# Row maxima carried into the stacked queries by one DMA per batch, in a four-layer cross-attention kernel

## The chip, the core and the metric

The kernel runs on one core of a Trainium2 chip. The metric is the device time of one execution in microseconds. The engines are TensorE (PE), VectorE (DVE), ScalarE (ACT), GpSimd (POOL) and SyncE (SP); SP and ACT also issue DMAs, each through a queue of its own.

## What is computed

Eight batches of 128 tokens and 128 features pass four attention layers, all f32, against a context of the same shape. Layers 0, 2 (with its cross part, "C") and 3 have 16 heads of 8 features; layer 1 has 16 heads of 64.

```python
# layer 0 (heads of 8, mask on the keys), then layer norm
scores = q @ k.T ; p = softmax(scores * scale + mask) ; x = LN(x + (p @ v) @ wo)
# layer 1 (heads of 64): x = x + attention(rms(x), ctx)
# layer 2: x = x + sa(LN(x))          causal, with a router that blocks 64-token blocks
#          x = x + ca(LN(x), ctx)     cross layer, C
#          x = x + relu(LN(x) @ w1 + b1) @ w2 + b2
# layer 3: x = LN(x + attention(x, ctx, ctx))
```

## The kernel before

**Exact products from bf16.** The 8-feature heads are too short for f32 matmuls to be cheap, so queries and keys are cut into three bf16 parts (`part_q`, `part_k`, with `rest_q`, `rest_k` between) and stacked: `qs` and `ks0`/`ks1` hold, for each head, 6 rows per feature slot (table `SLOTS`) in which a part stands opposite the part it must meet. The stacks are filled by DMAs (`stack_dma`, one per slot, six per group of batches) from SP's queue, for the first group of queries from ACT's. The seventh slot (`ROW_SLOT`) of `ks0` holds the mask (`kaug`) and meets ones in `qs`; the eighth is unused.

**The two passes.** The four attention parts 0, 2, C, 3 give 32 items (`N_ITEM`), one per batch and part, numbered n. For item n TensorE makes the scores with queries on the partitions (`pe_scores`, L311: 8 matmuls per half of the heads; the score pass). VectorE takes the negated row maxima (`dve_max`, L463). GpSimd cuts them into three bf16 parts (`pool_split`), TensorE turns them (`pe_mT`, L321), ScalarE copies them to `mrow` (`act_mrow`, L383). Then TensorE makes the scores a second time with keys on the partitions (L294; the shifted pass) and adds the maxima with 8 more matmuls of a selection matrix `sel` and `mrow` (L304), so that ScalarE's exponential (`act_exp`, L389) needs no bias per row. The probabilities then multiply the values (`pe_V`, L338), `act_osum` copies the result, `pe_back` turns it, `dve_norm` divides it by its sums, `pe_onT` turns it again, `act_onT` (L402) copies it, and `pe_z` (L355) multiplies it by the output matrix, `dve_z` adds the residual.

**Steps.** The order is written out by hand as steps s (`pe_attn`, `act_attn`, `dve_attn`, `pool_attn`). In step s the score pass of item s stands in both halves, with the second half of the shifted pass of item s-2 and the first half of that of item s-1; `pe_V` of item s-2 ends the step. Items from 24 on come one step later. `even` and `odd` put other work into the two halves: V chunks of layer 1 (`pe_v1`), projections, `pe_f1`, `pe_f2` and turns. Step 0 to 9 are layer 0; layer 1 (`pe_l1` and its like) follows with its own order; then steps 8 to 36 for layer 2, C and 3. The queries of an item of C or layer 3 come from the result of the layer before for the same batches, so each pair of batches has a chain: projection, parts, stack DMAs, score pass.

**Queues.** SP issues in the order of its program and waits for each part in turn: an issue behind a part that is not ready stands still. Input loads share the two queues with the stacks.

Of the kernel before, what the change touches and what calls it, by code (L numbers as in the profile page):

```python
# [7 lines left out]
P = 128  # L8
B = 8
# [27 lines left out]
ROW_SLOT = 6  # L37
HALVES = ((0, 4), (4, 4))
# [18 lines left out]
def build(nc, xt_d, x_d, ctxt_d, mask_d, wmat_d, wcol_d, wrow_d, out_d):  # L57
    ctx = ExitStack()
    with ctx:
# [50 lines left out]
        group = sb("group", [P, G])  # L110
        pick = sb("pick", [P, 8])
        sel = sb("sel", [P, 4, P], BF16)
# [14 lines left out]
        maskbc = xn[:, :, :].rearrange("p b t -> p (b t)")  # L127
        up = probs[:, 2, 0:HALF].bitcast(BF16).rearrange("p (b c) -> p b c", c=P)
# [91 lines left out]
        def data_of_S(n):  # L220
            L, b = layer(n), n % B
            return L.stacked("q", b) + L.stacked("k", b) + ([(sem("kaug_in"), 16)] if n == 0 else [])
# [14 lines left out]
        V1_EVEN = {1: (3,), 2: (6,), 3: (9,), 4: (11,), 5: (13,), 6: (15,)}  # L237
        V1_ODD = {0: (1, 2), 1: (4, 5), 2: (7, 8), 3: (10,), 4: (12,), 5: (14,)}
        freed(0, 1, sem("v_out_L1"), 1)
# [37 lines left out]
        def T_ready(e, n, half):  # L277
# [3 lines left out]
            if 2 * n + half:  # L281
                e.wait_ge(sem("exp_done"), 2 * n + half)

# [4 lines left out]
        def pe_scores(e, n, half, m, mhalf):  # L288

            if m is not None:  # L290
                M, b = layer(m), m % B
                T_ready(e, m, mhalf)
                for c, r, rows, i in heads(mhalf):
                    e.matmul(bank(4 + r)[:, bt(c)], ks[M.slot][rows, i, bt(b)], qs[rows, i, bt(b)],  # L294
                             start=(c == 0), stop=False, skip_group_check=True)
                if M is L2:
                    for a in range(2):
                        e.matmul(bank(4 + a), causal[:, :], identB[:, :].unsqueeze(1).broadcast_to([P, 4, P]),
                                 start=False, stop=False, skip_group_check=True)
# [23 lines left out]
        def pe_V(e, n):  # L323
            e.wait_ge(sem("exp_done"), 2 * n + 2)
            e.wait_ge(sem("vpad_in"), n + 1)
            if n >= 2:
                e.wait_ge(sem("z_read"), n - 1)
            if n == 0:
                e.wait_ge(*L0.v_done("v_out", 1))
            if n == 1:  # L330
# [1350 lines left out]
```

## Time and profile before

| | us |
|---|---|
| median of 3 runs | 361.03 (358.65 to 361.56) |
| profiled execution | 359.1 |
| its span | 357.3 |

| engine | busy us | share |
|---|---|---|
| PE, matmul | 308.4 | 86% |
| PE, weight load | 215.2 | 60% |
| DVE | 242.2 | 68% |
| ACT | 212.7 | 60% |
| POOL | 97.1 | 27% |

The span runs from the first to the last instruction. Busy shares are means over stages with different limits, so the stages are read apart. The first score pass starts at 19.48 us, step 2 at 31.05, layer 1 fills about 80 to 182, step 11 starts at 199.71, step 16 at 233.85, step 32 at 336.08. TensorE's granted clock is 0.981 of full speed over the span.

### The profile page before, as it was taken

The page shows a single profiled execution, that of the slowest core. Times are in us where ns is not written, and L with a number is a line of the kernel's source. Part 1 is how long each engine was busy: PE and PEld are TensorE (multiplying, and loading weights), DVE is VectorE, ACT ScalarE, POOL GpSimd, SP SyncE. Part 2 cuts the span into 40 slices and gives each one's busy share as a digit, 9 for nine tenths or more (in the row PEclk, how much of TensorE's full clock was granted, in tenths as well). Part 3 has the DMA queues.
Part 4 walks back from the last instruction along what each step waited for, and adds up shares of the span by engine and source line. Part 5 has one row for each costly group of instructions (what it writes and reads, how often), then busy time and mean ns, then how long its engine had stood idle before and what let it go on. Part 6 is the DMA issues. An engine that isn't in the chain of part 4 may idle for free.

```text
span 357.3 us, 10164 instructions
## 1 busy us (share of the span) xinstructions
PE 308.4 (86%) x4069; PEld 215.2 (60%) x4069; DVE 242.2 (68%) x478; ACT 212.7 (60%) x459; POOL 97.1 (27%) x263
## 2 busy tenths in 40 slices
PE   2779999997999999988879999989886977998871
PEld 0434566775778778867655556556654765775550
DVE  7656478628987467667657456868876647667755
ACT  2247767757785785876745645646574553556560
POOL 8011734310310000101405534233342313423231
PEclk9969999999999999999999999999999999999898
DMA  6447740000000000001311322412332010011000
GB/s 215 146 123 209 253 186 5 2 0 2 2 2 2 0 2 0 2 2 46 84 50 37 85 69 68 121 31 74 91 90 61 3 47 24 24 46 38 25 17 29
DMA packets 26158, 20.65 MB, mean 58 GB/s; under 512 B 3192, under 2 KB 24960, under 8 KB 25856
## 3 DMA queue, kind: packets, MB, share of 16 engines
q1 hardware_dynamic: 24656, 18.44, 17.6%
q10 hardware_dynamic: 1456, 1.58, 1.4%
q8 instruction: 32, 0.52, 0.6%
q14 instruction: 14, 0.11, 0.1%
HBM read 6.63 MB, written 0.52 MB: 20 GB/s over the span
## 4 chain that ended last, share of the span: by engine, by line
PE 50%; DVE 16%; ACT 12%; issue 6%; SPq 5%; DMA 5%; POOL 4%; ACTq 1%; POOLq 0%
SPq L653 5%; PE psum L338 5%; ACT probs L822 5%; PE psum L780 4%; DMA qs<-part_q 4%; PE psum L311 4%; PE psum L695 4%; PE psum L746 4%; PE psum L721 3%; ACT probs L830 3%; PE psum L294 3%; PE psum L304 3%; DVE maxs L463 3%; PE psum L757 2%; PE psum L941 2%
## 5 line engine op out<-in xcount | busy, mean ns | idle before, releaser
L463 DVE TENSOR_REDUCE maxs<-psum 128x8 f32<-128x1024 f32 x64 | 77.8, 1215 | 48.3 <-PE psum L311 32.2
L389 ACT ACTIVATE probs<-psum 128x1024 f32<-128x1024 f32 x64 | 65.5, 1023 | 36.5 <-PE psum L304 36.3
L311 PE MATMUL psum<-ks,qs 64*128 64x128 bf16 x512 | 26.0, 221 | 14.8 <-DMA qs<-part_q 8.0
L338 PE MATMUL psum<-probs,vpad 128*32 128x128 f32 x1024 | 35.4, 280 | 0.0
L822 ACT ACTIVATE probs<-psum,maxs 128x128 f32<-128x128 f32 x128 | 34.8, 391 | 0.5 <-DVE maxs L871 0.5
L338 PEld LDWEIGHTS psum<-probs,vpad 128*32 128x32 f32 x1024 | 26.7, 111 | 12.2 <-ACT probs L389 6.4
L441 POOL CAST mp<-maxs 128x16 bf16<-128x16 f32 x32 | 6.9, 216 | 91.1 <-DVE maxs L463 90.6
L524 POOL TENSOR_SCALAR rstd<-stats 128x2 f32<-128x2 f32 (+1 forms) x19 | 4.2, 223 | 100.6 <-DVE stats L490 100.5
L311 PEld LDWEIGHTS psum<-ks,qs 64*128 64x128 bf16 x512 | 15.1, 95 | 24.6 <-issue 9.7
L881 DVE TENSOR_REDUCE mres<-probs 128x8 f32<-128x1024 f32 x16 | 19.4, 1215 | 12.3 <-ACT probs L822 12.3
L871 DVE TENSOR_REDUCE maxs<-psum 128x8 f32<-128x1024 f32 x16 | 19.5, 1220 | 11.7 <-PE psum L746 11.7
L294 PE MATMUL psum<-qs,ks 64*128 64x128 bf16 x512 | 25.6, 220 | 0.6 <-ACT probs L389 0.6
L304 PE MATMUL psum<-mrow,sel 32*128 32x128 bf16 x512 | 25.3, 217 | 0.0
L294 PEld LDWEIGHTS psum<-qs,ks 64*128 64x128 bf16 x512 | 14.5, 94 | 13.6 <-issue 7.7
L304 PEld LDWEIGHTS psum<-mrow,sel 32*128 32x128 bf16 x512 | 14.4, 93 | 11.9 <-issue 6.6
L396 ACT COPY osum<-psum 128x256 f32<-128x256 f32 x32 | 12.0, 375 | 14.9 <-PE psum L338 14.6
L772 PE MATMUL psum<-probs,v1all 128*64 128x128 f32 x256 | 17.5, 279 | 3.4 <-ACT probs L830 2.9
L830 ACT COPY probs<-psum 128x1024 f32<-128x1024 f32 x16 | 16.7, 1042 | 6.2 <-PE psum L757 6.2
L885 DVE TENSOR_TENSOR probs<-probs,mres 128x1024 f32<-128x1024 f32 x16 | 19.6, 1225 | 0.6
L526 POOL TENSOR_TENSOR rstd<-rstd,small 128x2 f32<-128x2 f32 (+1 forms) x23 | 17.9, 780 | 1.9
L695 PE MATMUL psum<-wmat,ctxT 128*128 128x512 f32 x32 | 18.4, 676 | 0.0
L772 PEld LDWEIGHTS psum<-probs,v1all 128*64 128x64 f32 x256 | 13.7, 136 | 7.1 <-ACT probs L830 5.9
(154 smaller groups left out, 633.8 us busy)
## 6 DMA issues: line engine op xcount, KB each, us to landing
qs<-part_q SPq DMA_DIRECT2D x78, 64.0 KB, 2.0
ks<-part_k SPq DMA_DIRECT2D x30, 128.0 KB, 2.4
ks<-part_k SPq DMA_DIRECT2D x36, 64.0 KB, 2.0
wmat<-in_wmat SPq DMA_DIRECT2D x1, 1856.0 KB, 9.3
wmat<-in_wmat SPq DMA_DIRECT2D x1, 1024.0 KB, 5.1
qs<-part_q SPq DMA_DIRECT2D x6, 128.0 KB, 2.4
wrow<-in_wrow SPq DMA_DIRECT2D x1, 704.0 KB, 6.3
wmat<-in_wmat ACTq DMA_DIRECT2D x1, 512.0 KB, 8.2
```

The source lines that it names most:

```text
L294: e.matmul(bank(4 + r)[:, bt(c)], ks[M.slot][rows, i, bt(b)], qs[rows, i, bt(b)], start=(c == 0), stop=False, skip_group_check=True)
L304: mm = e.matmul(bank(4 + a)[:, bt(i)], sel[rg(j), i, :], mrow[rg(j), m % 2, :], start=False, stop=True, skip_group_check=True)
L311: s_mm = e.matmul(bank(2 * half + r)[:, bt(c)], qs[rows, i, bt(b)], ks[L.slot][rows, i, bt(b)], start=(c == 0), stop=L is not L2, skip_gro ...
L338: mm = e.matmul(o_bank(n)[rg(c), bt(half)], vpad[:, n % 2, 4 * half + c, G * a:G * a + G], pt, start=(a == 0), stop=(a == 1), skip_group_c ...
L389: e.activation(probs_of(n, half), bank(4, 2), ACT.Exp, scale=layer(n).scale)\
L463: e.tensor_reduce(maxs[:, n % 2, 8 * half:8 * half + 8], bank(2 * half, 2).rearrange("p (h k) -> p h k", k=P), AX.X, ALU.max, negate=True)\
L695: e.matmul(bank(to), ctxT[:, bt(c // 2)], mat("v1")[:, c % 2 * 512:(c % 2 + 1) * 512], start=True, stop=True).then_inc(L1("v_mm"), 1)
L772: mm = e.matmul(bank(6)[HD * pp:HD * pp + HD, bt(t)], v1[:, b, h * HD:(h + 1) * HD], pT[:, half, bt(4 * pp + t)], start=True, stop=True)
L822: ins = e.activation(probs[:, half, bt(s)], bank(2 * half, 2)[:, bt(s)], ACT.Exp, bias=maxs[:, b % 2, 8 * half + s:8 * half + s + 1])
L830: e.copy(pT[:, half, :], bank(4, 2)).then_inc(L1("pT_out"), 1)
L871: e.tensor_reduce(maxs[:, b % 2, 8 * half:8 * half + 8], bank(2 * half, 2).rearrange("p (h k) -> p h k", k=P), AX.X, ALU.max, negate=True)\
L885: e.tensor_tensor(p8, p8, rec.unsqueeze(2).broadcast_to([P, 8, P]), ALU.mult).then_inc(L1("norm"), 1)
```

## The change

The eighth slot (`MAX_SLOT`) of the keys' stacks now holds ones, and that of `qs` holds zeros during the score pass. When the maxima are turned and copied to `mrow`, ScalarE issues one DMA that writes them into this slot of `qs` for the batch. The shifted pass then adds them by itself; `sel`, `mrow`'s matmuls and the three VectorE instructions that made `sel` go. Because an item's maxima stay in the slot, it is cleared by a further DMA for each pair of queries of C and 3 (`clear_q`), and once for layer 2. Slot rows that fills of whole stacks wrote before are now filled by three DMAs from `resid` (`slots`), and the key stacks' fills between layers write ones instead of zeros.

The order moves with it. Both halves of item s-2's shifted pass stand in step s; `pe_V` is cut into halves at the end of step s and in the next; `pe_onT`, `act_onT` and `pe_z` of an item stand all in one step; the DVE order of `dve_norm`, `dve_z` and the second maximum changes. GpSimd waits for the mask parts before its fills. Values of layer 0 and V chunk 0 move behind the first score pass. The loads of the masks, `x`, `wrow`, `wcol`, `a1` and the rest of the weights move from SP's queue to ACT's, and `v1` from ACT's to SP's. SP issues key and query parts in turn.

```diff
+MAX_SLOT = 7
+            if n == 0:
+                ready += [(sem("kaug_in"), 16), (sem("slots"), 48)]
...
+            if half == 0:
+                e.wait_ge(sem(f"rows{n % 2}"), 16 * (n // 2 + 1))
...
-                e.wait_ge(sem("mT_read"), m + 1)
-                for i in range(4):
-                    for a in range(2):
-                        j = 2 * mhalf + a
-                        mm = e.matmul(bank(4 + a)[:, bt(i)], sel[rg(j), i, :], mrow[rg(j), m % 2, :],
...
+        ROWS_ON_ACT = range(N_ITEM)
+
+        def max_rows(e, n):
+
+            e.wait_ge(sem("mT_read"), n + 1)
+            e.dma_start(qs[MAX_SLOT::8, :, bt(n % B)], mrow[:, n % 2, :]).then_inc(sem(f"rows{n % 2}"), 16)
...
-                pe_scores(e, n, 0, n2, 1)
+                pe_scores(e, n, 0, n2, 0)
                 ahead(s)
                 if n1 is not None:
                     pe_mT(e, n1)
+                if n4 is not None:
+                    pe_onT(e, n4)
                 even(s)
                 if n3 is not None:
-                    pe_back(e, n3)
+                    pe_V(e, n3, 1)
                 if n4 is not None:
                     pe_z(e, n4)
-                pe_scores(e, n, 1, n1, 0)
+                pe_scores(e, n, 1, n2, 1)
                 if n3 is not None:
-                    pe_onT(e, n3)
+                    pe_back(e, n3)
                 odd(s)
                 if n2 is not None:
-                    pe_V(e, n2)
+                    pe_V(e, n2, 0)
...
+        def clear_q(e, L, b0, nb):
+
+            e.wait_ge(sem("exp_done"), 2 * B * (L.at - 1) + 2 * (b0 + nb))
+            e.dma_start(qs[MAX_SLOT::8, :, toks(b0, nb)], kaug[:, 0:nb * P]).then_inc(sem(f"q_clear{b0}"), 16)
...
+            e.wait_ge(sem("fill"), 2)
+            e.dma_start(ks0[MAX_SLOT::8, :, :], ones.bitcast(BF16)).then_inc(sem("slots"), 16)
+            e.dma_start(qs[ROW_SLOT::8, :, :], ones.bitcast(BF16)).then_inc(sem("slots"), 16)
+            e.dma_start(qs[MAX_SLOT::8, :, :], zeros.bitcast(BF16)).then_inc(sem("slots"), 16)
+            e.dma_start(wmat[:, c1:c2], wmat_d[:, c1:c2]).then_inc(sem("in_v1"), 16)
...
-            e.memset(qs[:, :, :].rearrange("p c t -> p (c t)").bitcast(F32), TWO_ONES).then_inc(sem("qs_one"), 1)
-            e.memset(wide_f32(ks0, 3), 0.0).then_inc(sem("ks0_zero"), 1)
+            e.wait_ge(sem("up"), 3)
...
-            e.memset(ks0[:, 0:4, :].rearrange("p c t -> p (c t)").bitcast(F32), 0.0).then_inc(sem("ks0_zero"), 1)
```

On TensorE, one middle step of layer 0 before, from its second shifted pass to the next step's:

```order
L304 MATMUL psum<-mrow,sel 128x128 x8
L311 MATMUL psum<-ks,qs 128x128 x8
L321 MATMUL psum<-identB,mp 128x128
L695 MATMUL psum<-wmat,ctxT 128x512
L346 MATMUL psum<-identF,osum 128x128 x2
L355 MATMUL psum<-wmat,onT 128x128
L294 MATMUL psum<-qs,ks 128x128 x8
L304 MATMUL psum<-mrow,sel 128x128 x8
L311 MATMUL psum<-ks,qs 128x128 x8
L351 MATMUL psum<-identF,onorm 128x128
L695 MATMUL psum<-wmat,ctxT 128x512
L338 MATMUL psum<-probs,vpad 32x128 x16
```

The same step now:

```order
L302 MATMUL psum<-qs,ks 128x128 x8
L313 MATMUL psum<-ks,qs 128x128 x8
L323 MATMUL psum<-identB,mp 128x128
L354 MATMUL psum<-identF,onorm 128x128
L722 MATMUL psum<-wmat,ctxT 128x512
L340 MATMUL psum<-probs,vpad 32x128 x8
L358 MATMUL psum<-wmat,onT 128x128
L302 MATMUL psum<-qs,ks 128x128 x8
L313 MATMUL psum<-ks,qs 128x128 x8
L349 MATMUL psum<-identF,osum 128x128 x2
L722 MATMUL psum<-wmat,ctxT 128x512
L340 MATMUL psum<-probs,vpad 32x128 x8
```

The matmuls on `sel` are gone, and the turn to `onT` (L351, now L354) stands at the head of the step whose `z` (L355, now L358) uses it, where before it stood half a step and a value pass earlier.

On ScalarE, the same step of layer 0 before:

```order
L396 COPY osum<-psum 128x256
L389 ACTIVATE probs<-psum 128x1024
L383 COPY mrow<-psum 128x128
L700 COPY v1all<-psum 128x512
L389 ACTIVATE probs<-psum 128x1024
L700 COPY v1all<-psum 128x512
L402 COPY onT<-psum 128x128
```

And now:

```order
L403 ACTIVATE probs<-psum 128x1024
L388 COPY mrow<-psum 128x128
L397 DMA qs<-mrow 16x8x128
L416 COPY onT<-psum 128x128
L727 COPY v1all<-psum 128x512
L410 COPY osum<-psum 128x256
L403 ACTIVATE probs<-psum 128x1024
```

The issue of the maxima's DMA stands between their copy and the copy of `onT`, which moved from the step's end to behind it.

On SP, the stacks of C and layer 3 before (512 columns are a group of four batches of keys, 256 a pair of queries):

```order
L653 DMA ks<-part_k 16x8x512 x12
L653 DMA qs<-part_q 16x8x256 x12
L653 DMA ks<-part_k 16x8x512 x6
L653 DMA qs<-part_q 16x8x256 x6
L653 DMA ks<-part_k 16x8x512 x6
L653 DMA qs<-part_q 16x8x256 x30
```

And now, down to the third pair of queries of C:

```order
L668 DMA ks<-part_k 16x8x512 x9
L674 DMA qs<-kaug 16x8x256
L668 DMA qs<-part_q 16x8x256 x6
L668 DMA ks<-part_k 16x8x512 x3
L674 DMA qs<-kaug 16x8x256
L668 DMA qs<-part_q 16x8x256 x6
L668 DMA ks<-part_k 16x8x512 x5
L674 DMA qs<-kaug 16x8x256
L668 DMA qs<-part_q 16x8x256 x6
```

The last part of a group of keys is issued behind a pair of queries instead of ahead of it, and a clearing DMA stands ahead of each pair.

## Rows read from the trace of the kernel before

**Rows 1.** Windows by stage: start:end, length, each engine's busy us (instructions), clock, DMA.

```profile
37.38:60.08 22.70, 22.36 (x369) 13.92 (x366) 16.23 (x37) 16.15 (x29) 11.76 (x28) 1.00 0.44 159
199.71:233.85 34.14, 34.14 (x511) 20.06 (x508) 22.65 (x44) 18.65 (x35) 13.20 (x39) 1.00 0.31 85
233.85:278.50 44.65, 37.63 (x664) 25.17 (x660) 34.09 (x68) 26.88 (x51) 15.86 (x49) 1.00 0.25 68
278.50:336.10 57.60, 50.32 (x812) 36.90 (x810) 37.88 (x82) 30.20 (x61) 16.66 (x53) 0.98 0.11 30
```

**Rows 2.** Waits of PE from 190 us on: total us, times, longest.

```profile
PE psum L311 <- DMA qs<-part_q: 8.0, 6, 2.5
PE psum L311 <- DVE rest_q L629: 2.7, 3, 1.1
```

**Rows 3.** Timeline of one step of layer 0: start, us, engine, instruction.

```profile
48.41 0.40 PE L294 MATMUL psum<-qs,ks 64*128 64x128 bf16 x8
...
48.74 0.40 PE L304 MATMUL psum<-mrow,sel 32*128 32x128 bf16 x8
...
49.18 1.02 ACT L389 ACTIVATE probs<-psum 128x1024 f32<-128x1024 f32 x1 [0.26 <-PE psum L304]
...
49.40 0.23 PE L321 MATMUL psum<-identB,mp 128*128 128x128 bf16 x1
...
49.46 1.08 PE L695 MATMUL psum<-wmat,ctxT 128*128 128x512 f32 x2
...
50.10 0.26 ACT L383 COPY mrow<-psum 128x128 bf16<-128x128 bf16 x1
50.38 0.38 PE L346 MATMUL psum<-identF,osum 128*128 128x128 f32 x2
...
53.02 1.08 PE L338 MATMUL psum<-probs,vpad 128*32 128x128 f32 x32
...
53.61 0.27 ACT L402 COPY onT<-psum 128x128 f32<-128x128 f32 x1
...
54.03 0.40 PE L294 MATMUL psum<-qs,ks 64*128 64x128 bf16 x8
```

**Rows 4.** The costliest groups: the matmuls that add the maxima.

```profile
L304 PE MATMUL psum<-mrow,sel 32*128 32x128 bf16 x512 | 25.3, 217 | 0.0
```

**Rows 5.** The line of the stacks, issues on ACT's queue: duration min/median/max in ns.

```profile
L653 ACTq DMA_DIRECT2D qs<-part_q x6: 614/622/768, 12.8 to 16.2; - x6
```

**Rows 6.** DMA issues: KB of each, median us from issue to landing.

```profile
qs<-part_q SPq DMA_DIRECT2D x78, 64.0 KB, 2.0
...
ks<-kaug SPq DMA_DIRECT2D x1, 256.0 KB, 3.2
...
xn<-in_mask SPq DMA_DIRECT2D x1, 128.0 KB, 6.3
...
r1p<-in_wmat SPq DMA_DIRECT2D x2, 32.0 KB, 8.0
...
wcol<-in_wcol SPq DMA_DIRECT2D x1, 9.0 KB, 2.7
```

**Rows 7.** Timeline of the start.

```profile
1.80 3.51 POOL L1019 MEMSET qs<- 128x4096 f32 x1
...
2.95 5.08 DVE L1452 CAST probs<-mu 128x128 bf16<-128x128 f32 x1
...
8.27 0.23 DVE L1456 CAST probs<-mu 128x128 bf16<-128x128 f32 x1
...
9.34 1.76 DVE L1462 MEMSET ks<- 128x2048 f32 x1 [0.38 <-issue]
...
11.02 0.36 DVE L585 TENSOR_TENSOR rest_k<-psum,xn 128x256 f32<-128x256 f32 x1
```

**Rows 8.** The chain that ended last, before step 22: the key part and the issues.

```profile
265.74 1.13 POOL part_k L641
267.46 0.60 SPq L653
```

More of the change, by code:

```diff
@@ L221, in data_of_S @@
             L, b = layer(n), n % B
-            return L.stacked("q", b) + L.stacked("k", b) + ([(sem("kaug_in"), 16)] if n == 0 else [])
+            ready = L.stacked("q", b) + L.stacked("k", b)
+            if n == 0:
+                ready += [(sem("kaug_in"), 16), (sem("slots"), 48)]
+            if n == B:
+                ready += [(sem("q_clear"), 32)]
+            if n >= 2 * B and b % 2 == 0:
+                ready += [(sem(f"q_clear{b}"), 16 * (n // B - 1))]
+            return ready
         FREED = {(0, 1): [(sem("kaug_out"), 1)],
@@ L321, in pe_mT, with pe_V @@
             e.transpose(m_turned(n), mp[:, n % 2, :], identB[:, :]).then_inc(sem("mT_mm"), 1)
[L323 to L330, printed above, removed]
[L331 to L340 removed]
+        def pe_V(e, n, half):
+            e.wait_ge(sem("exp_done"), 2 * n + half + 1)
+            if half == 0:
+                e.wait_ge(sem("vpad_in"), n + 1)
+                if n >= 2:
+                    e.wait_ge(sem("z_read"), n - 1)
+                if n == 0:
+                    e.wait_ge(*L0.v_done("v_out", 1))
+                if n == 1:
+                    e.wait_ge(*L0.mm_done("q_rest", 4))
+                if n == B:
+                    e.wait_ge(L1("z_read"), B)
+            for a in range(2):
+                for c in range(4):
+                    pt = probs_of(n, half)[:, bt(2 * c + a)]
+                    mm = e.matmul(o_bank(n)[rg(c), bt(half)], vpad[:, n % 2, 4 * half + c, G * a:G * a + G], pt,
+                                  start=(a == 0), stop=(a == 1), skip_group_check=True)
+            if half:
+                mm.then_inc(sem("V_mm"), 1)
         def pe_back(e, n):
@@ L405, in act_attn @@
             for s in steps:
-                n1, n2, n3 = at(s - 1, lo, hi), at(s - 2, lo, hi), at(s - 3, lo, hi)
+                n1, n2 = at(s - 1, lo, hi), at(s - 2, lo, hi)
+                n3, n4 = at(s - 3, lo, hi), at(s - 4, lo, hi)
+                first(s, 0)
+                if n2 is not None:
+                    act_exp(e, n2, 0)
+                if n1 is not None:
+                    act_mrow(e, n1)
+                if n4 is not None:
+                    act_onT(e, n4)
+                even(s)
                 if n3 is not None:
                     act_osum(e, n3)
-                first(s, 0)
+                first(s, 1)
                 if n2 is not None:
                     act_exp(e, n2, 1)
-                if n1 is not None:
-                    act_mrow(e, n1)
-                even(s)
-                first(s, 1)
-                if n1 is not None:
-                    act_exp(e, n1, 0)
                 odd(s)
-                if n3 is not None:
-                    act_onT(e, n3)
         def pool_v(e, n):
@@ L790, in pe_l1 @@
                 if b == 0:
+                    pe_onT(e, B - 1)
                     pe_z(e, B - 1)
@@ L1183, in _ @@
             pe_s1(e, 0, 1)
+            pe_onT(e, B - 2)
+            pe_V(e, B - 1, 1)
+            pe_z(e, B - 2)
             e.wait_ge(sem("exp_done"), 2 * B)
@@ L1186, in _ @@
             pe_back(e, B - 1)
-            pe_z(e, B - 2)
-            pe_onT(e, B - 1)
             def during1(b, place):
@@ L1441, in _ @@
             e.memset(up[:, :, :], 0.0).then_inc(sem("up"), 1)
+            e.memset(ones, TWO_ONES).then_inc(sem("fill"), 1)
+            e.memset(zeros, 0.0).then_inc(sem("fill"), 1)
             u = sem("mask_split")
```

187 lines of the change are left out of this document (93 added, 94 removed).

## The prediction

> **What bounds the kernel now.** I read the stage windows first [rows 1]. In layer 0 and in layer 2 TensorE is never idle: 22.36 busy of 22.70 us over steps 3 to 6, 34.14 of 34.14 over steps 11 to 15. So a step there lasts as long as its matmuls: 5.68 and 6.83 us. In the cross layer and layer 3 it is busy 37.63 of 44.65 and 50.32 of 57.60 us, that is 14.3 us idle. The waits of TensorE there [rows 2] put 8.0 us on the query stacks' transfers and 2.7 on VectorE's remainders. The stretch of layer 1 (80 to 182 us) holds none of the changed matmuls; I leave it as it is.
>
> One step of layer 0 [rows 3] shows what each piece takes. From 48.41 to 48.74 eight shifted-score matmuls pass (0.33 us), then the eight that add the maxima need the same 0.33 before the exponential starts at 49.18 and takes 1.02. The maxima copy takes 0.26, the step ends at 54.03: 5.62 us.
>
> **What goes.** All 512 matmuls on `sel` and `mrow` [rows 4]. Their 217 ns is the pipelined length; the spacing is 0.33 us for eight, so two halves cost 0.66 us per batch, 21 us over 32 batches. This is the ceiling of the steady gain, paid only where TensorE is what a step waits for.
>
> **What comes in its place, per batch.** ScalarE copies the turned maxima, waits for its own copy and issues a DMA. An issue on ScalarE's queue takes 0.61 to 0.77 us [rows 5]; with the wait I take 0.72. The transfer is 128 pieces of 256 bytes. No such transfer is in the trace. The query stacks (512-byte pieces, 64 KB) land in 2.0 us; the bias columns, 128 pieces of 72 bytes, in 2.7 [rows 6]. I take 2.0, as the size and the target tile are the same, and keep 2.7 as the bound; for less than 2.0 no row speaks. The Trainium skill (DMA: Bandwidth & Descriptors, Specifications) speaks against the change here: below 512 bytes a piece is read, modified and written, which would put the landing nearer to the 2.7 of the bias columns; by the row it is 2.0, by that reading some 0.7 more for each batch whose copy is waited for.
>
> Two loops follow from the new order.
>
> *The maxima loop.* Shifted pass 0.33, gap 0.11, exponential 1.02, copy 0.26, issue 0.72, landing 2.0, then the next batch's shifted pass: a step can't be shorter than 4.4 us. Layer 0, at 5.0 after the cut, and layer 2, at 6.2, lie above it, so there the transfer is hidden behind the second half of the step.
>
> *The late `onT`.* Before, ScalarE copied the turned output `onT` at the end of a step (53.61 in [rows 3]), and `pe_z` used it in the middle of the next, 2.5 us later. Now TensorE turns it at the head of a step, ScalarE copies it behind exponential, maxima copy and issue, and TensorE asks for it (`pe_z`) in the middle of the same step. Earliest: 0.33 + 0.11 + 1.02 + 0.26 + 0.72 + 0.27 + 0.1 = 2.8 us after the step's start. What TensorE has before it is two passes of 0.33, the turn of the maxima 0.07 (49.40 to 49.46), that of `onT` 0.2, the even filler, and 0.5 for half of the value pass (its whole is 53.02 to 54.03): 1.4 us plus the filler. The filler of layer 0 is a V chunk, 0.92 (49.46 to 50.38): wait 0.5. In layer 2, where both passes carry 0.54 of mask matmuls more, the wait is 0.8 in the steps without filler. In the cross layer and layer 3 it is 0.9 to 1.3 with a light filler, none with `pe_f2` or a full projection. Queued behind this wait are the second shifted and score passes, and so VectorE's second maximum.
>
> **The sum, stretch by stretch.**
>
> *Start.* The cast L1452 takes 5.08 us beside GpSimd's 3.51 us fill of `qs` and the fills behind it; its twin L1456 without them takes 0.23 [rows 7]. GpSimd now waits for the mask parts, and VectorE's 1.76 us fill of `ks0` is gone. That would free 4.85 + 1.76 = 6.6 us, but the first mask piece is issued at 1.6 and lands 6.3 later [rows 6], at 7.9, where L585 now starts at 11.02: 3.1 us. From L585 to the first scores the new order needs about 1.0 + 3.9 (six issues) + 0.6 + 3.2 (the `kaug` transfer [rows 6]) = 8.7, so 16.6 instead of 19.48. The three slot transfers (768 KB) and the 512 KB for `v1` ride ahead on the same queue and may eat all of that. From the first scores to step 2 (31.05 now, 11.6 us) the chain is two maxima 1.22 each behind the passes, GpSimd's split 1.4, turn, copy, issue and landing: 9.2. Sum -5.3; bounds 0 and -7.5.
>
> *Layer 0, steps 2 to 9.* Four steps have no such wait for `onT` (no `z` yet, or the 1.85 us chunks before it): 4 x -0.66; four have it: 4 x (-0.66 + 0.5). That is -3.3. The last value pass and its return come half a step later: +0.5. Together -2.8; bounds -5.3 and 0.
>
> *Layer 2.* Its first shifted pass now waits for copy, issue and landing (3.0 us) with only one score pass (0.9) and little else to cover it; less its own cut I charge +1.0. Steps 11 to 15: 5 x -0.66 + 0.8 x 3 - 0.3 = -1.2 with the waits partly covered by turns. With step 10's cut of 1.3: -1.5; bounds -4.6 and +1.
>
> *Cross layer and layer 3, steps 16 to 31.* Cut 15 x 0.66 = -9.9. The SP queue was in the way: at 265.74 GpSimd computes the last key part, at 267.46 the query stack's issues follow it [rows 8], though the query's first part, made in the step before, had been ready some 3 us. I lay 4.5 of the 8.0 us to this, which happened at steps 16, 20 and 22. The new order puts the late key parts behind the queries, and the added clearing DMA (some 0.6 us of SP) goes out before the part is ready, while SP is idle: -4.5. The other 8 us or so of short waits shrink by about half, since the new waits for `onT` stand in the same steps: -4.3. Against it nine light steps at +1.0: +9. In layer 3 the query stack is asked for one step after its projection, and that step gets shorter, so part of the cut turns into a wait there; I count it in the halving above. Sum -9.9 - 4.5 - 4.3 + 9.0 = -9.7; bounds -15 and -3.
>
> *End.* The last batch pays issue and landing in full, 2.7, less 0.33 of `sel`, some 0.5 of the value pass and some 0.5 as VectorE takes the second maximum before its other work: +1.3 (rounded); bounds +0.5 and +2.5.
>
> Sum: -5.3 - 2.8 - 1.5 - 9.7 + 1.3 = -18.0. The profiled execution took 359.1 us (span 357.3), so 341.1; the median of the three runs, 361.03, is 1.9 above it: **343 us**.
>
> **Rivals.**
> 1. *The wait for `onT` does not come* (ScalarE gets to it earlier, or the passes absorb it). Then the cut is whole: 0.5 x 4 in layer 0, 2 in layer 2, 4 more later, -8: 335. For it: TensorE has always other work queued; against: it is in order, and `z` stands ahead of the second pass.
> 2. *ScalarE's queue is the new bound.* Its waiting issue costs 1.2 us, not 0.72: the `onT` wait and both loops grow by 0.5 in some 20 steps, +10, or the start gives nothing (+5): 348 to 353. For it: in layer 0 ScalarE is busy 16.15 of 22.70 [rows 1] before the issue; against: the six issues in a row stay near 0.65.
> 3. *The row transfers land late* and the kernel gets slower. A step is then 2.4 + landing. It takes 18 us over 28 steps, 0.65 us on steps of about 5.8: from a landing of 4.0 us on the kernel is slower than before; at 4.5 it is 375. What speaks for it: a transfer behind a big load on the same queue waits for it, as `r1p` (32 KB) took 8.0 us behind the last load of `wmat` [rows 6], and exactly those loads move onto ScalarE's queue. The Trainium skill (DMA: Bandwidth & Descriptors, Queues, rings and completion order) says that each engine consumes one queue's descriptors in ring order; the row of `r1p` agrees. Against: they are issued one at a time (steps 3 and 5), and the next maxima follow about 5 us behind, when a load of that size is nearly down.
> 4. *It hardly moves*: the gains in the start and in the late layers are absorbed by other transfers, 357 to 364.
>
> **How the numbers follow.** Forecast (337 to 348) 0.52; rival 1 and better 0.15; rival 2 and a dull start 0.22; rival 4 0.05; rival 3 0.06. Range 333 to 354, which leaves out the two last and a thin slice of rival 1. Faster by over 1% (what a measurement of this kernel can tell) 0.89, within 1% 0.05, slower 0.06.
>
> **What would show it.** First scores at 16 to 17 us, and L1452's successor at 0.2 us. Layer 0 steps of 5.1 to 5.5 us with TensorE waiting about 0.5 for ScalarE's `onT` copy before `pe_z`; layer 2 steps near 6.6. ScalarE's row issues 0.6 to 0.8 us, landing 2.0 to 2.2, and no TensorE wait on them except for batches 0, 8 and the last. No wait over 1 us on `qs<-part_q` before steps 16, 20 and 22, but still one or two in layer 3. If steps in layers 0 and 2 are equal to before or TensorE waits for `qs<-mrow` in every step, rival 2 or 3 holds. A first score pass at 19 us or later breaks the first term.

## The result and the profile after

The changed kernel takes 370.44 us (median of 4 executions, 369.14 to 372.21), the kernel before beside it 359.84 (358.54 to 361.56): 1.0295 times as long, 95% interval 1.022 to 1.037. I had forecast 343, range 333 to 354. The profiled execution after has a span of 367.1 us against 357.3. Below, a ratio is always to the kernel before on the same chip; executions that the chip disturbed (a lower granted clock) are left out, and for one run (e2) only one of four is left.

The page's busy times of the kernel after (engine, us, share, instructions), then TensorE's five longest waits from 190 us on, to be read against [rows 2]:

```profile
PE 302.3 (82%) x3557; PEld 203.6 (55%) x3557; DVE 235.7 (64%) x476; ACT 212.2 (58%) x458; POOL 93.2 (25%) x262
```

```profile
PE psum L313 <- DMA qs<-part_q: 7.9, 4, 2.9
PE psum L358 <- ACT onT L416: 7.3, 14, 1.1
PE psum L567 <- DVE xn L558: 3.7, 4, 1.1
PE psum L313 <- DVE rest_q L644: 2.4, 5, 0.7
PE psum L313 <- DVE rest_k L644: 2.2, 4, 0.8
```

The 512 matmuls are gone, yet TensorE is busy only 6 us less, and waits where it did not: the waits for stacks are as long as before (7.9 against 8.0), and 7.3 us of waits for `onT` have been added (0.4 before). The windows by stage (start:end, length, busy us and instructions of PE, PEld, DVE, ACT, POOL, granted clock, DMA share, GB/s) answer to [rows 1]:

```profile
37.01:59.94 22.93, 21.35 (x305) 12.00 (x302) 15.36 (x35) 16.34 (x30) 11.35 (x26) 1.00 0.42 140
...
200.77:235.74 34.97, 32.64 (x431) 17.80 (x427) 22.03 (x42) 18.74 (x35) 12.44 (x36) 1.00 0.31 82
235.74:280.00 44.26, 36.43 (x537) 22.52 (x534) 34.06 (x69) 26.36 (x50) 16.61 (x51) 0.96 0.29 80
...
310.00:345.00 35.00, 27.98 (x397) 19.77 (x401) 21.44 (x44) 16.64 (x32) 9.39 (x32) 0.85 0.13 33
```

The same four steps of layer 0 take 22.93 us instead of 22.70, the same five of layer 2 34.97 instead of 34.14, both now with idle TensorE.

The start of the first score pass of an item n, read from the timelines of the profiled executions, shows where a kernel gains or loses (item 8 opens layer 2, 16 C, 24 layer 3; the last column is the span):

| | 0 | 8 | 16 | 24 | 31 | end |
|---|---|---|---|---|---|---|
| before | 19.48 | 181.89 | 236.35 | 293.00 | 337.00 | 357.3 |
| after | 19.48 | 182.26 | 237.13 | 295.52 | 344.18 | 367.1 |
| e1, before without the cut matmuls | 19.45 | 181.32 | 231.02 | 289.49 | 334.99 | 355.5 |
| e3, after without row transfers | 21.28 | 184.82 | 236.31 | 290.40 | 334.31 | 357.8 |
| e4, after, rows behind `onT` | 20.95 | 183.02 | 235.78 | 290.58 | 336.56 | 359.3 |
| e5, e4 with fewer issues | 20.69 | 183.89 | 235.78 | 289.67 | 333.00 | 355.6 |
| e11, e4 with the old SP order | 21.64 | 184.57 | 237.39 | 300.22 | 347.30 | 369.9 |
| e12, before with the new SP order | 19.43 | 181.50 | 234.66 | 288.53 | 331.32 | 352.4 |
| e15, e12 with a gated fill | 16.01 | 175.84 | 229.00 | 283.21 | 326.01 | 347.0 |

After against before: nothing at the start, +0.4 by layer 2, +0.8 by C, +2.5 by layer 3, +7.2 by the last item, +9.8 at the end. The loss is in the late layers and the tail. Each row is one execution. The start of the kernel after is kept in e3, e4, e5 and e11, and there the first scores come at 20.69 to 21.64 us: its 19.48 is the early end of what this start gives.

One step of layer 0 after, down to its second pass (start, us, engine, instruction), against [rows 3]:

```profile
54.13 0.40 PE L302 MATMUL psum<-qs,ks 64*128 64x128 bf16 x8
...
55.48 0.26 ACT L388 COPY mrow<-psum 128x128 bf16<-128x128 bf16 x1
...
55.77 0.55 ACTq L397 DMA_DIRECT2D qs<-mrow  x1
...
56.42 0.27 ACT L416 COPY onT<-psum 128x128 f32<-128x128 f32 x1 [0.68 <-ACT mrow L388]
...
56.74 0.30 PEld L358 LDWEIGHTS psum<-wmat,onT 128*128 128x128 f32 x2 [0.24 <-ACT onT L416]
...
57.16 0.40 PE L302 MATMUL psum<-qs,ks 64*128 64x128 bf16 x8
```

`onT`'s copy starts 0.68 us behind the end of the maxima copy, with the row's issue between them, `z` starts 2.6 us into the step (I had computed 2.8), and the second pass stands behind it. The row transfers themselves, by the line of their issue:

```profile
L397 ACTq DMA_DIRECT2D qs<-mrow x32: 539/540/550, 27.5 to 350.7; - x32
...
  PE psum L302: 1.5, 2
...
DMA to landing us min/median/max: 1.8/1.8/4.0
```

### The profile page after: what moved, and what is told of

It reads as the page before. It is cut to its first block, busy times and chain, and to the rows that moved or that the text cites. A ratio compares the mean times of both kernels' runs of the same rounds, so it can differ in the third digit from the quotient of the medians.

```text
span 367.1 us, 9213 instructions
## 1 busy us (share of the span) xinstructions
PE 302.3 (82%) x3557; PEld 203.6 (55%) x3557; DVE 235.7 (64%) x476; ACT 212.2 (58%) x458; POOL 93.2 (25%) x262
## 4 chain that ended last, share of the span: by engine, by line
PE 42%; ACT 17%; DVE 14%; issue 11%; DMA 6%; ACTq 4%; SPq 4%; POOL 2%; POOLq 0%; DVEq 0%
ACT probs L850 4%; DMA qs<-part_q 4%; PE psum L807 4%; PE psum L748 4%; PE psum L313 4%; PE psum L773 4%; SPq L668 4%; ACT probs L858 3%; ACTq L397 3%; PE psum L358 3%; PE psum L340 3%; PE psum L722 2%; PE psum L784 2%; PE psum L969 2%; DVE maxs L478 2%
## 5 line engine op out<-in xcount | busy, mean ns | idle before, releaser
L313 PE MATMUL psum<-ks,qs 64*128 64x128 bf16 x512 | 26.9, 227 | 23.4 <-DMA qs<-part_q 13.9
L340 PE MATMUL psum<-probs,vpad 128*32 128x128 f32 x1024 | 42.1, 283 | 0.3 <-DVE x L497 0.3
L313 PEld LDWEIGHTS psum<-ks,qs 64*128 64x128 bf16 x512 | 17.0, 98 | 38.2 <-issue 26.1
L340 PEld LDWEIGHTS psum<-probs,vpad 128*32 128x32 f32 x1024 | 24.5, 110 | 21.0 <-issue 11.2
L909 DVE TENSOR_REDUCE mres<-probs 128x8 f32<-128x1024 f32 x16 | 19.4, 1216 | 12.3 <-ACT probs L850 12.3
L497 DVE TENSOR_TENSOR x<-psum,resid 128x128 f32<-128x128 f32 x32 | 9.2, 288 | 23.0 <-PE psum L358 23.0
L358 PE MATMUL psum<-wmat,onT 128*128 128x128 f32 x64 | 16.0, 333 | 8.7 <-ACT onT L416 8.4
L416 ACT COPY onT<-psum 128x128 f32<-128x128 f32 x32 | 8.6, 269 | 19.8 <-ACT mrow L388 16.6
L358 PEld LDWEIGHTS psum<-wmat,onT 128*128 128x128 f32 x64 | 9.8, 193 | 16.5 <-ACT onT L416 15.3
L748 PE MATMUL psum<-xnT,wmat 128*128 128x256 f32 x64 | 17.4, 400 | 0.3 <-ACT ks L755 0.3
```

The costliest lines, as they stand in the source:

```text
L313: s_mm = e.matmul(bank(2 * half + r)[:, bt(c)], qs[rows, i, bt(b)], ks[L.slot][rows, i, bt(b)], start=(c == 0), stop=L is not L2, skip_gro ...
L340: mm = e.matmul(o_bank(n)[rg(c), bt(half)], vpad[:, n % 2, 4 * half + c, G * a:G * a + G], pt, start=(a == 0), stop=(a == 1), skip_group_c ...
L358: e.matmul(o_bank(n)[:, P:2 * P], onT[:, n % 2, :], mat(layer(n).o), start=True, stop=True).then_inc(sem("z_mm"), 1)
L748: mm = e.matmul(bank(chunk_bank(i, name, c))[:, t * PAIR:(t + 1) * PAIR], a1[:, 2 * (2 * c + t) + KIND[name], :], src[:, i * PAIR:(i + 1) ...
L909: e.tensor_reduce(sums, p8, AX.X, ALU.add).then_inc(L1("sum"), 1)
```

## The experiments

### e1: the cut alone

```diff
...
-                        mm = e.matmul(bank(4 + a)[:, bt(i)], sel[rg(j), i, :], mrow[rg(j), m % 2, :],
-                                      start=False, stop=True, skip_group_check=True)
```

> The kernel before without the 512 matmuls that add the maxima; the waits stay, the maxima are still cut, turned and copied, and the softmax is left unshifted. It prices the cut alone, in the old order. If my step model is right (0.33 us for each half, paid in full in layers 0 and 2 and in part in the late layers), the time falls by 12 to 18 us, to 342 to 348. Rival (the cut is not worth its spacing, since the queue of TensorE, the clock or the waits behind it take it back): less than 6 us, 354 or more.

356.92 us, ratio 0.981 (0.975 to 0.988): 5.8 us below the 362.73 of before. The table shows the cut paid nearly in full in layer 2, where TensorE was busy: from item 8 to 16 49.7 us instead of 54.5, 0.6 for each step. Then it comes back: 16 to 31 takes 103.97 us against 100.65. In layer 0 the middle steps take 4.93 us instead of 5.62, the full 0.7, and yet item 8 comes only 0.6 us sooner: the granted clock stood at 0.50 from 24 to 30 us, where before it was at 1.00 from 27 us on, so that item 2 came 1.7 us later (33.56 against 31.89), and TensorE waited 2.9 us longer in all for the V chunks' copies and `onorm`. The rival holds for the late layers and for layer 0 as a whole, my model for layer 2. TensorE's waits from 233 to 340 us in e1 (in [rows 2] the stack and `rest_q` rows are 8.0 and 2.7 us):

```profile
PE psum L306 <- issue: 8.3, 4, 3.0
PE psum L306 <- DVE rest_q L624: 3.7, 3, 1.4
PE psum L306 <- DMA qs<-part_q: 2.7, 2, 1.9
```

Four waits of the score pass carry no releaser ("issue"); they stand, up to 3.0 us long, at first passes of pairs, where the stack is asked for. With the rows of stacks and remainders they make 14.7 us against 10.7. So in C and layer 3 the chain behind a pair sets the time, and fewer matmuls lengthen the wait for it. That is not all of it: TensorE was granted 0.92 of full speed over items 16 to 31, against 0.98 before (the table at e8), so its matmuls took 5.2 us less there and not 9.9. How much of the 3.3 us the clock alone took was not tried apart.

### e2 and e3: the new order with the old matmuls, and without either

```diff
-        ROWS_ON_ACT = range(N_ITEM)
+        ROWS_ON_ACT = ()
-                e.wait_ge(sem(f"rows{n % 2}"), 16 * (n // 2 + 1))
+                e.wait_ge(sem("mT_read"), n + 1)
```

(e2 has this edit and the matmuls on `sel` of before.)

> The kernel after, in its new order, but with the matmuls of before adding the maxima and no row transfers (the selection matrix holds zeros here, so the softmax is unshifted; the matmuls, the copy of the maxima and the waits have the size and place of before). It tells the order from the transfers. Theory O (the new order of the steps is what costs; the row transfer is cheap): the sel matmuls come back on top, 376 to 388. Theory R (ScalarE's row issue and the landing are what costs, some 0.6 us a step): cut and transfers cancel, 366 to 372.

> The kernel after without its 32 row transfers (the shifted pass waits for the copy of the maxima; the softmax is unshifted). It prices issue and landing together in the new order. Theory R: ScalarE no longer makes the copy of onT late (TensorE waited 8.4 us for it) and the layer-3 pairs lose 0.54 us from their chain once or twice: 352 to 360. Theory O: the waits of TensorE stay, only the issue goes: 364 to 369.

e2: 370.13 us against 362.73 before. That is the value that Theory R forecast (366 to 372), but it rests on one execution and settles little. e3: 356.78 us, ratio 0.986 (0.979 to 0.993). Beside e1 this is the closest comparison: both lack matmuls and row transfers, one in the old order (0.981), one in the new (0.986). All that the new order, the fills and the clears change is +0.5%, within the two intervals. This is a net figure: it holds SP's new order, which alone is worth 1.3% in the old steps (e12), so the other changes of the order cost more than 0.5%. The row transfers are the rest: from 0.986 to 1.0295, some 15 us. Theory R.

### e4: the row's issue behind the copy of `onT`

```diff
                 if n4 is not None:
                     act_onT(e, n4)
+                if n1 is not None:
+                    max_rows(e, n1)
```

(and `max_rows` leaves `act_mrow`.)

> The kernel after with the issue of the row transfer moved behind the copy of onT on ScalarE, so the copy of onT comes 0.6 to 0.7 us earlier in the step and the rows are sent 0.3 us later. Theory R: TensorE's waits of 8.4 us for onT shrink to below 1, and the time falls by 6 to 10 us, to 360 to 364, with the waits for the rows still near 1.5 us. Theory O: less than 3 us, 367 or more, since what TensorE saves there it waits for elsewhere (maxima, remainders, stacks).

362.74 us, ratio 0.999 (0.996 to 1.002), 3.0% below the kernel after. What waits for ScalarE's copy of `onT`, after and then e4 (who waited, us, times):

```profile
  PE psum L358: 8.4, 17
```

```profile
  PE psum L358: 1.9, 4
```

TensorE's wait falls by 6.5 us, to the 1.9 that e3 has too, and the time by some 11. More than the wait comes back. The chain of the pairs is not the reason: in e4 too the row's issue (at 312.02 us, 0.54) stands in it, ahead of the first part of the queries. What differs in the traces is the clock: of three dips in the late layers (at 276, 312 and 340 us) one is left, and over items 16 to 31 TensorE is busy 81.63 us instead of 85.85 for the same matmuls (e8). So of the 15 us, 11 belong to the place of the issue and 4.6 (0.986 to 0.999) to the issue itself.

### e7: the issue alone, in the old order

```diff
             e.copy(mrow[:, n % 2, :], m_turned(n)).then_inc(sem("mT_read"), 1)
+            e.wait_ge(sem("mT_read"), n + 1)
+            e.dma_start(kaug[:, bt(n % B)], mrow[:, n % 2, :]).then_inc(sem(f"rows{n % 2}"), 16)
```

> The kernel before with one more transfer of 32 KB per batch, 128 pieces of 256 bytes, issued by ScalarE behind its copy of the maxima into a tile that nobody reads; no engine but ScalarE itself (two batches later) waits for it. It prices the issue alone in the old order. Theory R (0.54 us more on ScalarE in each step are on the path, whatever the order): +4 to +10 us. Theory O (only behind the new order, where onT and z follow in the same step, does the issue hurt): below +2.

365.94 us against 361.86, ratio 1.012 (1.005 to 1.019): +4 us, with an issue of 0.47 us and nobody who reads what it moves. That is the 1.3% between e3 and e4 again, in the other order: 32 x 0.5 us of ScalarE, a quarter of it on the path.

### e5, e10, e13, e14: is it the chain of the pair?

In the kernel after, from one pair of layer 3 to the next (start, us, what):

```profile
311.67 2.74 PE psum L969 x16
...
316.00 0.73 POOL rstd L541
...
317.51 0.41 PE psum L567 x2
...
318.06 0.27 ACT mrow L388
...
318.36 0.54 ACTq L397
...
319.00 0.48 ACT part_q L621
...
319.50 0.53 SPq L668
...
322.00 0.61 SPq L668
...
322.65 2.06 DMA qs<-part_q
...
324.75 0.40 PE psum L313 x8
```

From the score pass of the pair at 310.62 to that at 324.75 the chain never rests: second feed-forward matmuls, residual, layer norm, turn, then ScalarE's copy of the maxima and the row's issue, then the first part of the queries, five of SP's six issues in a row (3.1 us) and 2.06 of landing. Before, the chain of the pair at 318.64 went from the projection straight to ScalarE's part; its pairs were 12.7 and 13.0 us apart (305.91, 318.64, 331.60); here they are 14.1 and 13.6.

e5 leaves two of the six issues out:

```diff
+                if L is L3 and name == "q" and n in (1, 2):
+                    continue
```

> The kernel of the run before (row issue behind the copy of onT) in which the query stacks of layer 3 issue four transfers instead of six (two of the three copies of part 0 are left out, so layer 3's products are incomplete). SP's chain for a pair gets 1.2 us shorter. Theory C (from step 24 on the pair's chain, from the second feed-forward matmuls through layer norm, projection, parts, SP's issues and landing to the score pass, sets the step, not TensorE's matmuls): the pairs from 26 on each come 1.2 us sooner, 3 to 5 us in all, 358 to 360. Rival (TensorE's work sets it): 0 to 1.

356.53 us, ratio 0.985 (0.979 to 0.991), against 0.999 for e4: 5 us by the ratios; the spans of the profiled executions differ by 3.7, and the three gaps between the pairs of layer 3 shrink by 1.8, 0.9 and 1.0 us. The chain of the pair sets the layer.

e10 takes the first part ahead of the maxima copy and the row (on the light start of e6):

```diff
+                part_first = lo and 24 <= s <= 30 and s % 2 == 0
+                if part_first:
+                    even(s)
```

> The light start again, with ScalarE in layer 3's even steps taking the first part of the queries ahead of the maxima copy, onT and the row issue. Theory C (the pair's chain sets layer 3's steps): 0.8 to 1.1 us less in the chain of each of three or four pairs, -2 to -4 us against the light start, 356 to 358. Rival (the rows and onT, now later, hold TensorE): same or +2.

359.07 us, ratio 0.993 (0.989 to 0.997); e6 has 0.994. No gain beyond noise: the copy and the issue, 0.8 us, are out of the chain, but TensorE waits 3.9 us for rows and 3.0 for `onT`, where e4 has 1.2 and 1.1:

```profile
PE psum L304 <- DMA qs<-mrow: 3.9, 3, 2.0
```

e13 and e14 let ScalarE issue two of the six, with and without the first part ahead, and load its table early.

```diff
+            for n in (1, 2):
+                e.dma_start(qs[n::8, :, toks(b0, nb)], part_q[:, 0, toks(b0, nb)]).then_inc(sem(f"qs{b0}"), 16)
```

> The kernel with the light start and the first part taken ahead of the maxima copy, with two more edits: ScalarE loads its table at the very start (it stood in the first chain, 1.28 us), and issues two of the six query stack transfers of each pair of layer 3 itself. Theory C: 1.2 us less on SP's part of the chain of four pairs, 0.5 to 1 us back through ScalarE, and 1.0 at the start: 3 to 5 us below the same kernel without them, 354 to 356. Rival (ScalarE's two issues delay part 1 of the queries and the exponential by as much): 358 to 360.

> The same two edits on the kernel with the light start alone, where the maxima copy, onT and the row issue stay ahead of the first part. Here the rows are early (no wait for them), but the chain of the pair has 0.9 us more. Theory C: 1 to 2 us behind the run with the first part ahead. Rival (rows that come late cost as much as the chain gains): equal to it.

Ratios 1.002 (0.997 to 1.006) and 0.999 (0.994 to 1.004): both rivals hold, and e13's 362.03 us lie above the 358 to 360 of its own, although the table now loads early. Two more issues keep ScalarE from `osum` in e13:

```profile
PE psum L352 <- ACT osum L411: 7.1, 4, 2.6
```

SP's issues and ScalarE's are one budget here: what leaves SP's part of the chain returns through ScalarE.

### e9: GpSimd issues the rows

```diff
+                if n1 is not None:
+                    max_rows(e, n1)
                 extra(s)
```

(in GpSimd's order, on e6.)

> The kernel with the light start (row issue behind onT) in which GpSimd issues the row transfers on its own queue, ahead of its cutting of the next maxima, instead of ScalarE. Theory R (ScalarE's 0.54 us a step are what is left of the loss): the time goes to that of the kernel without row transfers, -3 to -5 us against the light start, 355 to 357. Rival (GpSimd's issue is slow, or delays its cut of the maxima and so the turn): same or slower, +1 to +10.

361.66 us, ratio 0.998 (0.992 to 1.004): no better than e6. ScalarE is free, but GpSimd stands still in front of the issue:

```profile
L397 POOL DMA_DIRECT2D qs<-mrow x32: 525/560/739, 25.8 to 342.3; - x32
...
  ACT mrow L390: 37.4, 27
```

37.4 us of waiting in which its norms and parts can't run. The gain that e3 promises would need an engine that has nothing else to do; SP's queue was not tried for the rows.

### e8: is it the clock?

The granted clock of TensorE in the kernel after, in windows around two of its dips. Ahead of the first stand three waits of 0.6 to 1.1 us (two for `onT`, one for a layer norm), ahead of the second one of 2.5 for a stack:

```profile
272.00:276.00 4.00, 2.35 (x53) 1.58 (x46) 3.00 (x6) 2.12 (x5) 2.64 (x8) 1.00 0.21 54
276.00:280.00 4.00, 4.00 (x27) 3.24 (x27) 2.45 (x6) 1.83 (x4) 1.04 (x5) 0.58 0.04 8
...
336.00:340.00 4.00, 1.66 (x26) 1.15 (x26) 1.85 (x4) 1.18 (x2) 1.43 (x6) 0.68 0.20 53
340.00:344.00 4.00, 3.94 (x50) 2.38 (x44) 2.69 (x8) 1.66 (x3) 0.37 (x2) 0.50 0.04 8
```

After a window with 2.35 of 4 us busy the next is granted 0.58 of full speed; after 1.66 it is 0.50, the lower of the two levels, 1.2 GHz, and the feed-forward matmuls at 311.67, in a third dip, take 2.74 us, where those of the next pair take 1.79. The run puts six dummy matmuls ahead of each pair's score pass from item 20 on, where the waits are:

```diff
+            if busy:
+                for _ in range(6):
+                    e.matmul(bank(0), identB[:, :], identB[:, :].unsqueeze(1).broadcast_to([P, 4, P]),
+                             start=True, stop=True, skip_group_check=True)
```

> The kernel after with six matmuls of 512 columns (1.3 us in all at the full clock), whose results are overwritten, in front of TensorE's wait for each pair's query stack from item 20 on (six places). Theory K (the waits of 2 to 3 us there are followed by a granted clock of half speed for 2 to 4 us, which makes the matmuls behind them twice as long): the dips at 276, 311 and 336 to 345 us shrink, time -2 to -5 us. Rival (the clock dips cost nothing, or the extra matmuls only delay): 0 to +3.

370.24 us against 361.86, ratio 1.024 (1.018 to 1.031), where the kernel after has 1.0295 (1.022 to 1.037): the intervals overlap. The same windows in e8:

```profile
276.00:280.00 4.00, 3.40 (x53) 2.42 (x52) 2.32 (x6) 2.09 (x5) 1.03 (x3) 1.00 0.04 9
...
340.00:344.00 4.00, 3.40 (x74) 2.30 (x70) 3.11 (x6) 1.93 (x5) 0.00 (x0) 1.00 0.04 8
```

These dips are gone, the loss is not: the items still come late by 4.8 at item 25 and 6.7 at item 31. But the run is no clean price of the clock. At items 20 and 22 the stack was there in time, and the dummy matmuls push the score pass back by 1.4 us each; and behind item 31 the clock falls instead (0.77 to the end, 0.87 in the kernel after). The stretch from item 16 to item 31 in the profiled executions (idle is the length less the busy time):

| | us | TensorE busy | idle | granted clock |
|---|---|---|---|---|
| before | 100.65 | 87.59 | 13.06 | 0.98 |
| e1 | 103.97 | 82.35 | 21.62 | 0.92 |
| e3 | 98.00 | 81.23 | 16.77 | 0.98 |
| after | 107.05 | 85.85 | 21.20 | 0.94 |
| e4 | 100.78 | 81.63 | 19.15 | 0.98 |
| e8 | 105.87 | 89.08, dummies included | 16.79 | 1.00 |
| e11 | 109.91 | 86.28 | 23.63 | 0.92 |

The kernels after, e3, e4 and e11 make the same matmuls here, and at 0.92 to 0.94 they take 4 to 5 us more than at 0.98. In e8 the stretch is 1.2 us shorter than in the kernel after, though 2.8 us of dummies were in the way. From both I estimate that the dips cost some 4 us of the 6.4 lost here. They are no cause of their own: they come where TensorE waits, and e3 and e4, which take the waits away and leave the clock alone, are rid of two of the three.

### e6: the start

```diff
+            slots(0, PAIR)
             stack_up(e, L0, "k", 0, 2)
             e.wait_ge(sem("kaug_out"), 1)
             e.dma_start(ks0[ROW_SLOT::8, :, :], kaug[:, :]).then_inc(sem("kaug_in"), 16)
+            e.dma_start(wmat[:, c1:c2], wmat_d[:, c1:c2]).then_inc(sem("in_v1"), 16)
+            slots(PAIR, T)
```

> The kernel with the row issue behind the copy of onT, and a lighter start: the slot transfers fill only the first pair's columns ahead of the first stacks (192 KB instead of 768), the rest and the 512 KB of v1 follow behind them. If the transfers ahead in the queues ate my start gain (the query stacks landed 5.6 us after their issue instead of 2.1), the first scores come 2.5 to 4 us sooner, at 16 to 18.5 us, and the time falls by 2 to 4. Rival (something else sets 19.5, the table load and ScalarE's parts): first scores at 19 or later, time the same.

359.88 us, ratio 0.994 (0.990 to 0.997) against 0.999 of e4. The start of the kernel after shows why mine did not come (timeline; GpSimd now waits, so the cast is short, as forecast, and the remainder starts at 7.04 instead of 11.02):

```profile
3.00 0.23 DVE L1500 CAST probs<-mu 128x128 bf16<-128x128 f32 x1
...
7.04 0.42 DVE L600 TENSOR_TENSOR rest_k<-psum,xn 128x256 f32<-128x256 f32 x1 [2.88 <-DMA xn<-in_mask]
...
7.55 1.28 ACT L621 ACT_TABLE_LOAD   x1 [7.55 <-DVE rest_k L600]
...
10.09 3.93 ACTq L668 DMA_DIRECT2D qs<-part_q  x6
...
19.48 0.61 PE L313 MATMUL psum<-ks,qs 64*128 64x128 bf16 x8 [6.00 <-DMA qs<-part_q]
```

The stacks' last issue ends at 14.0 and lands at 19.4. The transfers of the first 20 us (KB each, us to landing), of the kernel after and then of e10, which starts as e6 does:

```profile
qs<-resid SPq DMA_DIRECT2D x2, 256.0 KB, 9.4
wmat<-in_wmat SPq DMA_DIRECT2D x1, 512.0 KB, 10.9
...
qs<-part_q ACTq DMA_DIRECT2D x6, 64.0 KB, 5.6
```

```profile
qs<-part_q ACTq DMA_DIRECT2D x6, 64.0 KB, 2.1
```

With the light start the query stacks land in 2.1 us again, and the first scores start at 16.45 in e10 and at 16.91 in e9 (e6's own profiled execution has 18.13).

### e11 and e12: SP's order, in the new steps and in the old

> The kernel with the row issue behind onT (start as in the kernel after), SP's stacks of C and layer 3 issued in the order of before (keys whole ahead of the queries). My sum gave SP's new order 4.5 us. If so, this is 3 to 5 us slower than with the new order, 365 to 367. Rival (the pair's chain is not held by the key issues): within 1.5 us of 362.

> The kernel before with nothing changed but SP's order of the stacks of layers 2, C and 3 (key and query parts in turn, the last key parts behind a pair of queries). My sum laid 4.5 us of the kernel before's 8.0 us waits to the old order. If that holds for the old steps too: -3 to -5 us, 357 to 359. Rival (the old order of the steps leaves SP enough time, and only the new steps with the clears and the later maxima need the new order): within 1.5 us of before.

```diff
-            stack_up(e, LC, "k", 4, 4)
+            stack_dma(e, LC, "k", 4, 4, 0)
             stack_up(e, LC, "q", 0, 2)
+            stack_dma(e, LC, "k", 4, 4, 1)
+            stack_dma(e, LC, "k", 4, 4, 2)
```

(e12, with the like for the other stacks, those of layer 2 too; e11 undoes it for C and layer 3.) e11: 374.35 us, ratio 1.038 (1.028 to 1.049) against 0.999 for e4, some 14 us slower. e12: 355.74 us against 361.45, ratio 0.987 (0.981 to 0.994): 4.6 us faster. My 4.5 was right for the old steps (between items 16 and 31 the profiled execution is 4.0 us shorter); in the new ones the order is worth three times that. In e11's chain three of the four pairs of C wait for GpSimd's cut of the maxima, its last key part (at 229.65, 255.03 and 268.92 us, 1.13 each) and then SP's clear and six issues. The clock takes part: it is 0.92 from item 16 to 31, and the matmuls there take 4.7 us more than in e4. Why the order weighs more in the new steps than in the old was not tried apart. The stacks' waits of TensorE from 190 us on, e11 and then e12:

```profile
PE psum L313 <- DMA qs<-part_q: 14.5, 7, 2.9
```

```profile
PE psum L311 <- DMA qs<-part_q: 3.5, 3, 1.8
```

### e15: the two gains, without rows

```diff
+            e.wait_ge(sem("up"), 3)
             e.memset(qs[:, :, :].rearrange("p c t -> p (c t)").bitcast(F32), TWO_ONES).then_inc(sem("qs_one"), 1)
```

(on e12: one wait on GpSimd.)

> The kernel before in its old steps, with SP's new order of the stacks and one more edit of the start: GpSimd waits for the mask parts before it fills the query stack (the one edit of my start term that does not need the new steps). Start theory: VectorE's cast takes 0.23 instead of 5.08 us, the first remainder starts near 8 instead of 11.02, first scores at 16.5 to 17.5 instead of 19.48; with the 4.6 us of SP's order, 352 to 354. Rival (GpSimd's fill now runs beside VectorE's own fill of the keys and slows it as it slowed the cast): first scores at 19 or later, 355 to 357.

350.94 us (6 executions, 348.85 to 353.71) against 362.71, ratio 0.974 (0.968 to 0.980). It keeps the matmuls on `sel` and beats both kernels; the start and SP's order add up. The start gives more than the 3.4 us of the first scores: step 2 begins at 24.97 us, 6.1 sooner than before, for the most part because the matmuls between run at the full clock (the four of the V chunk behind the first scores take 1.98 us, before 3.78).

```profile
3.03 0.23 DVE L1459 CAST probs<-mu 128x128 bf16<-128x128 f32 x1
...
4.25 3.51 POOL L1026 MEMSET qs<- 128x4096 f32 x1 [2.39 <-DVE probs L1467]
...
4.56 1.76 DVE L1469 MEMSET ks<- 128x2048 f32 x1 [0.37 <-issue]
...
6.63 0.42 DVE L585 TENSOR_TENSOR rest_k<-psum,xn 128x256 f32<-128x256 f32 x1 [0.30 <-DMA xn<-in_mask]
```

VectorE's own fill takes 1.76 us beside GpSimd's as it did alone; only the cast had suffered, 5.08 us in [rows 7]. The Trainium skill (SBUF — State Buffer, SBUF: two separate sides) says that a VectorE operation in a mode that takes both ports and a GpSimd operation exclude each other for a whole instruction. A cast that waits agrees with it, and more than it says: in the kernel before the cast lasted from 2.95 to 8.03 us, through GpSimd's whole run of fills (1.80 to 7.95) and not only the one under way.

## Why the prediction was wrong

The sum was -18.0 us; the spans of the profiled executions differ by +9.8.

**Start, -5.3 against 0.** The cause was right (the cast 0.23, the remainder 4 us sooner, more than the 3.1 I allowed), and I had named the slot transfers and `v1` as what may eat it all, but took -5.3. They ate it: 5.6 us of landing against 2.1. A smaller step was overlooked: ScalarE's table load, hidden before by its fill of the keys, came onto the chain (1.28 us). Without that traffic the first half of the term is there: first scores at 16.45 (e10) and 16.01 (e15), where I had 16.6. The second half, 9.2 us instead of 11.6 from there to step 2, is not: it takes 11.6 in the kernel after and 12.5 in e10. I had added up the chain of the maxima and put at nothing the matmuls that the change moves into this stretch, the values of layer 0, at half clock there (2.07 us for eight, before 1.05 ahead of the first scores).

**Layer 0, -2.8 against 0.** The stretch from step 2 to layer 1 (31.05 to 79.84 before, 31.08 to 80.01 after) is unchanged. I had charged 2.0 us of waits for `onT`, and TensorE waits 0.3. What ate the cut is TensorE's own time (busy 44.94 us instead of 47.26, for some 4.8 of matmuls less) and 2.5 us more of other short waits. The value pass in halves, and turns and `z` that stand alone between waits, take more than as one run (0.57 to 0.60 for each half against 1.01 for the whole, 0.42 for `z` against 0.32, 0.27 to 0.36 for the first turn against 0.21): in layer 2 a step of before without a wait took 6.64 us (227.21 to 233.85), and after the cut of 0.66 and with a wait of 0.68 it is not 6.66 but 7.18 (228.56 to 235.74).

**Layer 2, -1.5 against +0.4** (items 8 to 16). Cut alone -4.8 (e1). In the new order with nothing sent it is -3.0 (e3), with the rows sent -1.7 (e4), and with them ahead of `onT` +0.4. I had the wait for `onT`, not the cost of the issue itself, which I laid beside TensorE's work.

**C and layer 3, -9.7 against +6.4** (item 16 to 31). This is the step that failed: "Cut 15 x 0.66 = -9.9". I had read 14.3 us of idle TensorE and still paid the whole cut there. The cut in the old order loses 3.3 us in this stretch (e1): idle time grows by 8.6 us, because the pair's chain, not TensorE, ends last, and the clock falls with it; e5 shows the chain from the other side, 5 us for eight issues less. The other fault is `onT`, which I charged to TensorE alone (+9.0) where it waits 3.2 us: the cost is not there but in ScalarE's queue, where the maxima copy and the row's issue stand in the chain ahead of the first part, and in the clock, which I had left at full speed: by the estimate at e8 some 4 us. The SP term was right in size where I had read it (e12), but the new steps need the new order to stand still at all (e11).

**End, +1.3 against +2.6.** From the last item's scores to the end: 20.3 us before, 22.9 after, 23.5 without rows (e3). TensorE waits for no row transfer in it, but 2.4 us for `onT`. So it is not the landing that I charged but the order: value pass, return, turn and `z` of the last items come up to a step later.

**The rivals.** Rival 3 (rows land late) is refuted: 1.8 us at the median, 4.0 at worst, TensorE waits 1.5 us for them in all. The transfer is half the size of a stack's, not the same size as I wrote. Its pieces of 256 bytes did not land later than the stacks' 512 bytes (2.0), so the Trainium skill's rule (DMA: Bandwidth & Descriptors, Specifications) of a read-modify-write below 512 bytes shows no cost here. Rival 2 had the right place and the wrong mechanism and size: the issue costs 0.54 us, less than my 0.72, and still ScalarE's queue decides (e3, e4, e7), through what stands behind it. None of my rivals ended above 364 us with the transfers quick: that outcome had no chance of its own.

## What to carry to other kernels

Before paying a cut, ask in each stage what ends last there: take the work out and leave all else as it is, as e1 did; where TensorE was already idle, the cut was worth nothing or less here. Read the granted clock beside every such run: short waits lowered it here, and the matmuls behind them took longer. An issue of half a microsecond on a compute engine is an instruction like any other: price what is queued behind it, and put it behind what another engine waits for, not ahead. When several edits come in one change, the ones that need no other (here SP's order and one wait at the start) can be worth more than the idea they were made for.

## What I had not expected of the hardware

A transfer of 128 pieces of 256 bytes between tiles landed in 1.8 us, quicker than the stacks' 64 KB at 2.0. The stacks' landing tripled (2.1 to 5.6 us) behind 1.28 MB of slot rows and values' weights on SP's queue, with the loads on ScalarE's. TensorE's clock fell to half speed in the late layers at 276 us, behind three waits of 0.6 to 1.1 us, and at 312 and 340, behind waits of 2.9 and 2.5. Six dummy matmuls ahead of each pair kept it up, but where no wait stood they cost 1.4 us each time, and the time hardly moved.
